# One more tile of distance between scores and transposes in the layer-2 attention of a four-layer network

## The reference, cut to what matters

```
qp = einsum('bld,ed->ble', q, Wq)              # q is layernorm(x)
scores = einsum('bld,bmd->blm', qp, kv)
idx = argmax(scores, axis=-1)                  # the context row that each token picks
mem = take_along_axis(kv, idx[..., None], axis=1)
mk, mv = split(einsum('bld,ed->ble', mem, Wkv), 2, axis=-1)
logits = einsum('bhld,bmd->bhlm', qh, mk) * scale
attn = softmax(logits, axis=-1)
out = einsum('bhlm,bmd->bhld', attn, mv)
x = x + einsum('bld,ed->ble', out, Wc)
```

## Time and profile before

| | |
|---|---|
| time, median of 3 runs (lowest to highest) | 3002.34 us (3000.97 to 3005.05) |
| time of the profiled execution | 3000.7 us |
| its span, first to last instruction | 2999.1 us |
| granted TensorE clock over the span | 0.941 of full |
| PE busy over the span | 2573.6 us |
| DVE busy over the span | 2191.7 us |
| ACT busy over the span | 1411.2 us |

### The profile page before, as it was taken

The page is one execution under the profiler, slowest core; times in us unless marked ns, Lnnn a source line. Parts: engine busy times, 40 slices in busy tenths (PEclk is TensorE's granted clock), DMA queues, the critical chain, the costliest instruction groups (busy, mean ns, idle before and its releaser), DMA issues. The chain is left out here.

```text
span 2999.1 us, 67269 instructions
## 1 busy us (share of the span) xinstructions
PE 2573.6 (86%) x24770; PEld 1866.3 (62%) x24798; DVE 2191.7 (73%) x5427; ACT 1411.2 (47%) x2523; POOL 440.0 (15%) x542
## 2 busy tenths in 40 slices
PE   5957669995899999999999689896979776999578
PEld 4734346663887887887887466664756554555337
DVE  6889869997567767677676288887861186999764
ACT  3658868884011111111110377764643344777564
POOL 0012210000000000000000000000431253555104
PEclk9977879997999999999999699998999899999799
DMA  3110000002113113112111000000012220000001
GB/s 94 35 65 1 0 23 16 14 10 100 70 57 114 58 57 113 57 56 106 65 56 57 17 16 12 14 4 29 29 36 90 89 78 22 1 0 0 1 0 56
DMA packets 55559, 128.97 MB, mean 43 GB/s; under 512 B 9716, under 2 KB 21460, under 8 KB 54616
## 3 DMA queue, kind: packets, MB, share of 16 engines
q1 hardware_dynamic: 47864, 106.41, 10.4%
q0 software_dynamic: 7520, 20.34, 2.2%
HBM read 109.41 MB, written 17.30 MB: 42 GB/s over the span
## 5 line engine op out<-in xcount | busy, mean ns | idle before, releaser
L1500 PE MATMUL banks<-l1f_feed,l1f_w 128*128 128x512 f32 x512 | 228.2, 596 | 1.4 <-DVE l1f_feed L1769 1.4
L1443 PE MATMUL banks<-l1f_sums,l1f_mixes 128*128 128x256 f32 x768 | 186.6, 379 | 0.0
L1769 DVE TENSOR_TENSOR l1f_feed<-l1f_aoT,l1f_rwb 128x512 f32<-128x512 f32 x256 | 158.8, 682 | 16.2 <-PE banks L1443 10.4
L1500 PEld LDWEIGHTS banks<-l1f_feed,l1f_w 128*128 128x128 f32 x512 | 95.6, 191 | 108.5 <-issue 89.9
L1443 PEld LDWEIGHTS banks<-l1f_sums,l1f_mixes 128*128 128x128 f32 x768 | 146.0, 190 | 19.9
L1735 DVE TENSOR_TENSOR l1f_sums<-l1f_feed 128x512 f32<-128x512 f32 x128 | 88.5, 691 | 87.9 <-PE banks L1443 84.1
L1443 PE MATMUL banks<-l1f_feed,l1f_mixes 128*128 128x256 f32 x512 | 135.3, 387 | 19.2 <-DVE l1f_feed L1726 19.2
L214 POOL COPY x<-xn 128x512 f32 (+1 forms) x16 | 9.7, 609 | 933.7 <-DVE xn L1786 933.7
L1463 PE MATMUL banks<-l1f_w,l1f_feed 128*128 128x128 f32 x1024 | 136.8, 277 | 0.0
L836 POOL TENSOR_TENSOR l3a_kbd<-l_kT,consts 128x1024 f32<-128x1024 f32 x64 | 121.4, 1897 | 64.5 <-PE banks L871 63.8
L1463 PEld LDWEIGHTS banks<-l1f_w,l1f_feed 128*128 128x128 f32 x1024 | 126.3, 194 | 0.0
(11 more groups left out here) (531 smaller groups left out, 7064.5 us busy)
## 6 DMA issues: line engine op xcount, KB each, us to landing
l1f_rwb<-l1f_shares SPq DMA_DIRECT2D x128, 512.0 KB, 6.6
l0a_ctxT<-in_ctxT SPq DMA_DIRECT2D x16, 256.0 KB, 2.6
l2f_sent<-l0f_zero SPq DMA_DIRECT2D x4, 1024.0 KB, 7.0
l1a_ctxT<-in_ctxT SPq DMA_DIRECT2D x16, 256.0 KB, 2.6
l2c_ctxT<-in_ctxT SPq DMA_DIRECT2D x16, 256.0 KB, 2.6
l2e_rows<-l2f_sent SPq DMA_DIRECT2D x16, 256.0 KB, 2.7
l2f_answers<-l2e_y POOLq DMA_DIRECT2D x16, 256.0 KB, 2.7
l3p_ctxT<-in_ctxT SPq DMA_DIRECT2D x16, 256.0 KB, 2.7
```

The source lines that it names most:

```text
L1443: return pe.matmul(prods[:, n, :], left, right, start=(p == 0 and first), stop=(p == PAIRS - 1), skip_group_check=True)
L1500: pe.matmul(out_bank, w[:, 1, e, :], feed[:, e % NB, :], start=(e == 0), stop=(e == E - 1)).then_inc(s.y_psum, 1)
L1769: dve.tensor_tensor(feed[:, e % NB, :], aoT[:, m, :], rwb[:, m, e, :], ALU.mult).then_inc(s.ae_ready, 1)
```

## The change

The parts from the transposes on move one step back, each with the engine that follows it: `turn` and `copy_pT` from lag 15 to 16, `weigh` and `normalise` from 16 to 17, `project` and `add_x` from 17 to 18, `stats_x` and `copy_mv` from 18 to 19. `score`, `centre`, `exp` and all parts once a group keep their lags, the order of the lists stays, and `prob` gets four buffers (two more of 128 x 1024 f32), so that `centre` of tile t waits for the transposes of tile t - 4. Layer 1, which uses the same class, keeps two buffers and its lags.

```
-    def __init__(self, nc, k, ctx, s, name, softmax_scale, bias=None, v_pairs=H // 2):
+    def __init__(self, nc, k, ctx, s, name, softmax_scale, bias=None, v_pairs=H // 2, probs=2):
...
-        self.prob = sb("prob", [P, 2, H, S])
+        self.prob = sb("prob", [P, probs, H, S])
...
-                                self.prob[:, r % 2, 2 * n:2 * n + 2, :], self.k.ident[:, :])
+                                self.prob[:, r % self.probs, 2 * n:2 * n + 2, :], self.k.ident[:, :])
...
-        all_heads = self.prob[:, r % 2].rearrange("p a n -> p (a n)")
+        all_heads = self.prob[:, r % self.probs].rearrange("p a n -> p (a n)")
...
-        wait(dve, s.pT_psum, t - 1)
-        dve.tensor_tensor(self.prob[:, r % 2], self.scores, self.top[:, :].unsqueeze(2).to_broadcast([P, H, S]),
+        wait(dve, s.pT_psum, t - self.probs + 1)
+        dve.tensor_tensor(self.prob[:, r % self.probs], self.scores, self.top[:, :].unsqueeze(2).to_broadcast([P, H, S]),
                           ALU.subtract).then_inc(s.centred, 1)
...
-        core = AttentionCore(nc, k, ctx, s, "l2a", float(HD) ** -0.5, v_pairs=2)
+        core = AttentionCore(nc, k, ctx, s, "l2a", float(HD) ** -0.5, v_pairs=2, probs=4)
...
-            pipeline(pool, k.NT, [(18, lambda t, r: core.copy_mv(pool, t, r)), (10, at_group(keep_q))], unroll=RING, behind=8)
+            pipeline(pool, k.NT, [(19, lambda t, r: core.copy_mv(pool, t, r)), (10, at_group(keep_q))], unroll=RING, behind=8)
...
-            pipeline(pe, k.NT, [(14, lambda t, r: core.score(pe, t, r)), (15, lambda t, r: core.turn(pe, t, r)),
-                                (17, lambda t, r: core.project(pe, t, r)), (16, lambda t, r: core.weigh(pe, t, r)),
+            pipeline(pe, k.NT, [(14, lambda t, r: core.score(pe, t, r)), (16, lambda t, r: core.turn(pe, t, r)),
+                                (18, lambda t, r: core.project(pe, t, r)), (17, lambda t, r: core.weigh(pe, t, r)),
                                 (3, at_group(turn)), (4, at_group(queries)), (5, at_group(choose)), (7, at_group(turn_hot)),
                                 (8, at_group(values)), (9, at_group(keys))], unroll=RING, behind=8)
...
-            pipeline(act, k.NT, [(15, lambda t, r: core.copy_pT(act, t, r)), (14, lambda t, r: core.exp(act, t, r)),
+            pipeline(act, k.NT, [(16, lambda t, r: core.copy_pT(act, t, r)), (14, lambda t, r: core.exp(act, t, r)),
...
-            pipeline(dve, k.NT, [(14, lambda t, r: core.centre(dve, t, r)), (16, lambda t, r: core.normalise(dve, t, r)),
-                                 (17, lambda t, r: core.add_x(dve, t, r)), (6, at_group(choose)), (8, at_group(store_v)),
-                                 (18, lambda t, r: core.stats_x(dve, t, r)), (15, at_group(spread_v))],
+            pipeline(dve, k.NT, [(14, lambda t, r: core.centre(dve, t, r)), (17, lambda t, r: core.normalise(dve, t, r)),
+                                 (18, lambda t, r: core.add_x(dve, t, r)), (6, at_group(choose)), (8, at_group(store_v)),
+                                 (19, lambda t, r: core.stats_x(dve, t, r)), (15, at_group(spread_v))],
                      unroll=RING, behind=8)
```

More of the change, by code:

```diff
@@ L1004 @@
 class AttentionCore:
-    def __init__(self, nc, k, ctx, s, name, softmax_scale, bias=None, v_pairs=H // 2):
+    def __init__(self, nc, k, ctx, s, name, softmax_scale, bias=None, v_pairs=H // 2, probs=2):
         def sb(n, shape, dt=F32):
             return ctx.enter_context(nc.sbuf_tensor(f"{name}_{n}", shape, dt))
-        self.k, self.s, self.scale, self.bias, self.v_pairs = k, s, softmax_scale, bias, v_pairs
+        self.k, self.s, self.scale, self.bias, self.v_pairs, self.probs = k, s, softmax_scale, bias, v_pairs, probs
         self.wo = sb("wo", [P, D])
```

## The result

The changed kernel takes 3039.27 us (median of 4 runs, 3037.54 to 3040.31), the kernel before 3001.65 (4 runs, 3000.91 to 3005.05): a ratio of 1.0121 with a 95% interval of 1.0109 to 1.0133. It is slower by 37.6 us, in the forecast's direction and within its range, but above the 3027 forecast. The profiled execution took 3037.54 us.

A forecast was written before the change was run, and what follows sets the result against it. No engine alone was the limit; the hand-over between PE and DVE set the 21.56 us group. Statistics 14.4 + clock 11.2 - ends 0.4 = 25.2 us on 3000.7 gave 3025.9, so 3027 us for the median, range 3013 to 3040.

The forecast's parts named there:

- The wait that goes: PE's transposes waiting for `exp`: at most 2.4 us of waits could come off, at least nothing; taken as 0.
- The statistics on the ring: `stats_x` lands on DVE in step 2, ahead of the maximum of step 3: 12 groups x 1.20 = 14.4 us.
- the ring: One group: 1.16 (score to maximum) + 8.79 (DVE) + 0.14 + 11.47 (PE, steps 0 and 1) = 21.56 us.
- The clock: PE's wait before the score of step 0 grows to about 3.0 us; 8 more clock falls x 1.4 = 11.2 us.
- the rival that had all falls do so: TensorE's clock stays low for more than one stretch, 8 more falls at 2.5 to 3.1 us: 3036 to 3042, chance 0.1.
- The ends: Phase start 1.08 and some 0.3 us less, drain about 1.01 us more for one copy: together -0.4 us.
- The steady clock: Rival: statistics cost 14 to 18 us on DVE, at most 3 more clock falls: 3016 to 3020, chance 0.17.
- no change: Rival: moved statistics hidden because DVE's maximum of step 3 waits for its score; only the ends left: 3002, chance 0.07.
- faster: Rival: the transposes' wait for `exp` is the bound; without it groups drop to PE's 19.43 us: 2976, chance 0.05.

The follow-up runs named there:

- the experiment that has the later transposes without the statistics' cost: Changed kernel with query matmuls moved to the end of step 3 and `stats_x`, `copy_mv` at lag 21 (step 0): 2997.30 us (0.9967 to 0.9987).
- the filling: Changed kernel with four extra matmuls on constants a group on PE at the end of step 3, in its wait: 3031.37 us (1.0068 to 1.0112).
- the experiment on step 0: Changed kernel with `stats_x` and `copy_mv` at lag 21 instead of 19, so the statistics fall in step 0: 3014.01 us, ratio 1.0032.
- the one with the queries moved: Changed kernel with query matmuls moved from step 0 to the end of step 3 and `copy_hT` ahead of `exp`: 3010.68 us (1.0014 to 1.0035).
- the half-filled one: Changed kernel with two extra matmuls on constants a group on PE at the end of step 3, instead of four: 3027.89 us, ratio 1.0074.
- the kernel before with the queries moved: Kernel before with query matmuls moved from step 0 to the end of step 3 and `copy_hT` ahead of `exp`: 2991.44 us, ratio 0.9957.

## Why the prediction was right, and where a term was too small

**The wait that goes** was rightly put at nothing. PE's waits of L1056 for `exp` left the list and the weight loads' fell from 31.1 to 16.3 us, without a gain; the experiment that has the later transposes without the statistics' cost shows the same from outside, -12.5 us with them and without them.

**The statistics on the ring** were right in place and size: 12 x 1.20 = 14.4 us forecast, 12 x 1.17 = 14.0 measured. Moving them alone makes the kernel about as slow as the whole change (+36.1 for +37.6 us), and with the clock held at 1.00 by the filling a group is 1.17 us longer, which was forecast as 22.8 us for a group without a fall (21.56 + 1.17 = 22.73).

**The clock** was the right mechanism and mis-sized: 8 x 1.4 = 11.2 us forecast, 20.8 measured. Three parts of the product were off. Of the waits, 12 of 12 were followed by a fall, where 9 of 12 were taken from gaps all over the trace; that is 11 new falls, not 8. A short fall cost 1.4 to 1.6 us, so that at 1.4 it was taken at its low end; the group that was read closely had 24.18 us, which the prediction gave as about 24.2. And 3 of the 11 were long, at 2.8 us; the rival that had all falls do so gave 3036 to 3042, which is where the time is, but 8 of 11 did not. Forecasting from a count of other gaps was the weak step: those stood between other work, and the experiments show that a gap's length alone does not tell whether a fall follows.

The wait itself was forecast at 3.0 us and is 2.70 to 2.87. The 1.2 us of statistics are in it, the 0.2 us of the transposes are not: PE's turns in step 3 now wait 0.28 us for ACT (L1979), so PE's work ends that much later and its wait for `centred` is shorter. This moves an idle time from one place to another and costs nothing.

The Trainium skill (TensorE: Matmul & The Clock Gate, "Why this matters for your kernels") gives gaps of more than about 3 us as what to avoid; the trace disagrees with that as a limit, since all 11 new falls stand behind waits of 2.70 to 2.87 us, and in the experiment on step 0 three stood behind 1.59 to 1.64 us.

**The ends** were forecast at -0.4 us, -1.4 at the start and +1.0 in the drain. They are +2.7: -0.4 at the start, 0.5 in the last scores, 2.6 in the drain. At the start the first weighing did leave step 16, but PE runs that step at 0.79 of full clock where it had 1.00, with the score at 1.99 us for 1.09, so that the step is 0.36 us shorter and not 1.08. In the drain the copy of the last tile but one does stand behind the last `exp`, as forecast, but the last transposes do not wait for it. What the step missed is `add_x`. The end of the changed kernel's phase, from the timeline:

```profile
2090.69 0.99 ACT L1094 COPY l2a_pT<-banks 128x1024 f32<-128x1024 f32 x1
2090.80 0.68 DVE L1126 TENSOR_TENSOR x<-x,banks 128x512 f32<-128x512 f32 x1
...
2091.62 0.46 PE L1082 MATMUL banks<-l2a_wo,l2a_oT 128*128 128x128 f32 x2 [1.12 <-DVE x L1126]
...
2093.08 1.09 PE L1056 MATMUL banks<-consts,l2a_prob 128*128 128x128 f32 x8
...
2094.21 1.02 ACT L1094 COPY l2a_pT<-banks 128x1024 f32<-128x1024 f32 x1 [2.53 <-PE banks L1056]
```

`add_x` of the last group but one moved to step 1 of its group, there behind the last subtraction and the normalising of DVE; the first projection of the last group waits 1.12 us for it, and the last transposes stand behind that projection on PE, so that the last copy waits 2.53 us (1.18 before). The copy that was forecast as the cost ends at 2091.68, 1.4 us before these transposes. From the last score to the last transposes it is 7.02 us instead of 5.07, of which 1.12 is that wait; the rest of the 2.6 was not taken apart. The prediction counted `add_x` as hidden, which it is in the middle of the phase, and did not follow it into the last group.

**The rivals.** The steady clock would have had to show 1.00 in the middle of the phase, which of the kernels with the statistics on the ring only the filled ones and the one with the queries moved did; no change and faster fell with the maximum of step 3, which has no idle time before it. The sum with the measured sizes is 14.0 + 20.8 + 2.7 = 37.5 us, for 37.6 by the medians.

## What to carry to other kernels

Where two engines take turns, draw the ring first, and ask of each moved instruction which side it lands on: 1.2 us of statistics cost nothing in a step where DVE waits and 1.17 us a group in one where PE waits for DVE, while an idle time of 31 us at weight loads was worth nothing. A wait behind which TensorE's clock falls has a second price beside its own length, here larger than the first; useful work of the same engine moved into the wait (the queries) gave back nearly as much as the statistics cost, and no fall came up to step 64. And a part that is hidden in every group has to be followed through the last one, where the work that hid it is gone.

## What the runs showed of the hardware that was not expected

**Falls of the clock do not follow the wait's length alone.** With the statistics on step 0, 3 of 11 waits of 1.53 to 1.70 us were followed by a fall, one of them of 1.59 us, while three others of 1.59 us behind the same work were not. Waits of 1.85 to 2.02 us, with 1.03 us more of matmuls ahead of them, were followed by none in 11. No run here settles the condition.

**The last phase of the program has two rhythms.** Its code is the same in all kernels, yet it takes about 74 to 75 us in most profiles and 80 to 83 in three. DVE's scaling there, by line, first of the changed kernel, then of the half-filled one (16 instructions; busy us, mean ns):

```profile
L2529 DVE TENSOR_SCALAR l3d_f<-l3d_f 128x2048 f32<-128x2048 f32 x16 | 20.9, 1304 | 22.6 <-ACT l3d_f L2516 22.6
```

```profile
L2533 DVE TENSOR_SCALAR l3d_f<-l3d_f 128x2048 f32<-128x2048 f32 x16 | 28.6, 1790 | 16.2 <-ACT l3d_f L2520 16.2
```

And the timeline of the half-filled one there:

```profile
2963.19 1.23 DVE L2533 TENSOR_SCALAR l3d_f<-l3d_f 128x2048 f32<-128x2048 f32 x1 [0.47 <-ACT l3d_f L2520]
2964.74 1.28 POOL L206 TENSOR_TENSOR xb<-x,l3f_b_out 128x512 f32<-128x512 f32 x1
2968.36 2.47 DVE L2533 TENSOR_SCALAR l3d_f<-l3d_f 128x2048 f32<-128x2048 f32 x1 [1.55 <-ACT l3d_f L2520]
2968.46 1.28 POOL L206 TENSOR_TENSOR xb<-x,l3f_b_out 128x512 f32<-128x512 f32 x1
```

Where it meets POOL's addition of 1.28 us DVE takes 2.47 us instead of 1.23, about the sum of both. (In the kernel before with the queries moved, two such meetings went the other way: POOL took 2.13 and 2.15 us, and DVE 1.28 and 1.23.) In the changed kernel this happens once; in the half-filled one it happens in 7 of 16, and then every second group until the end. The Trainium skill (SBUF — State Buffer, "Who interferes with whom") says that DVE in some modes and GpSimd share a pair of ports that one of them holds for its whole instruction; the trace agrees, with 2.47 us for 1.23 and 1.28. In which mode DVE worked here no run shows. The filled kernels' totals lie 7 to 9.5 us above what their phases explain (+27.6 and +24.7 against +18.1 and +17.6), and in their profiled executions the last phase has 7 to 9 of them; that it is so in their other runs as well was not seen, and what sends a run into the one rhythm or the other stays open.
